# Threshold search for top-k attention: the last counting round shared by three engines, with a new instruction timetable

## What is computed

```python
top_k = max(1, int(s * 0.2))                      # s = 512, so 102
threshold = lax.top_k(scores, top_k)[0][..., -1:]
emphasis = jnp.where(scores >= threshold, 1.24, 1.0)
scores = scores * emphasis
```

## Time and profile before

| | |
|---|---|
| median of three runs | 2922.21 us |
| the profiled execution | 2924.21 us |
| its span | 2923.0 us |
| granted TensorE clock, mean | 0.874 of full speed |
| busy: PE, DVE, ACT, POOL | 75%, 80%, 50%, 41% |

### The profile page before, as it was taken

The page is one execution under the profiler, slowest core; times in us unless marked ns, Lnnn a source line. Parts: engine busy times, 40 slices in busy tenths (PEclk is TensorE's granted clock), DMA queues, the critical chain, the costliest instruction groups (busy, mean ns, idle before and its releaser), DMA issues.

```text
span 2923.0 us, 33653 instructions
## 1 busy us (share of the span) xinstructions
PE 2182.0 (75%) x8767; PEld 1101.9 (38%) x8767; DVE 2338.2 (80%) x6145; ACT 1463.2 (50%) x3124; POOL 1189.6 (41%) x1118
## 2 busy tenths in 40 slices
PE   4169776978778876888679876888769887778645
PEld 2016222553234522554235522454235532355214
DVE  5884898979898798978998798978989788953472
ACT  2406723766166733767056742757146751644323
POOL 2020253615454253725445152724445163724461
PEclk8589798999989998989989999989989898789757
DMA  4001112242043312233033321333133321313223
GB/s 107 0 15 36 29 37 85 80 107 75 27 122 71 104 50 72 91 96 93 27 107 75 105 60 54 109 78 103 31 97 83 101 63 39 113 38 111 83 75 95
DMA packets 137459, 215.11 MB, mean 74 GB/s; under 512 B 17872, under 2 KB 57440, under 8 KB 134112
## 3 DMA queue, kind: packets, MB, share of 16 engines
q1 hardware_dynamic: 133088, 203.88, 24.2%
q0 software_dynamic: 4096, 8.40, 0.9%
HBM read 190.06 MB, written 22.15 MB: 73 GB/s over the span
## 4 chain that ended last, share of the span: by engine, by line
DVE 35%; issue 19%; PE 19%; POOL 10%; ACT 9%; DVEq 4%; DMA 3%; SPq 1%; POOLq 0%; ACTq 0%
DVE wmask L804 10%; DVE best L946 6%; DVEq L948 4%; POOL gat L1649 4%; PE ps_att L1064 3%; ACT wmask L786 2%; POOL slots L1765 2%; PE ps_rest L1353 2%; PE ps_rest L1439 2%; PE ps_att L1075 2%; PE ps_rest L1792 1%; DVE pick L953 1%; POOL rest_c L1662 1%; POOL rest_c L1649 1%; DVE hg L1621 1%
## 5 line engine op out<-in xcount | busy, mean ns | idle before, releaser
L1413 POOL TENSOR_TENSOR gat<-sil,cbs 128x512 f32<-128x512 f32 x256 | 324.4, 1271 | 137.0 <-ACT sil L1378 74.2
L1378 ACT ACTIVATE sil<-ps_rest,w_b1T 128x512 f32<-128x512 f32 x256 | 175.3, 685 | 383.3 <-PE ps_rest L1353 369.9
L804 DVE TENSOR_SCALAR_CACHE_REDUCE wmask<-z,tc 128x512 bf16<-128x512 f16 x512 | 345.8, 742 | 18.3 <-ACT z L771 15.6
L980 POOL TENSOR_SCALAR wmask<-wmask 128x512 bf16<-128x512 bf16 x256 | 158.2, 618 | 412.4 <-DVE wmask L937 409.2
L1064 PE MATMUL ps_att<-z,Vp 128*32 128x128 f32 x2048 | 277.3, 280 | 13.1 <-DVE z L1136 13.1
L1353 PE MATMUL ps_rest<-rest_hT,WF 128*128 128x512 f32 x512 | 281.5, 636 | 0.0
L1343 PE MATMUL ps_rest<-gat,WP 128*128 128x512 f32 x512 | 269.3, 608 | 15.6 <-POOL gat L1413 15.4
L737 PE MATMUL ps_att<-qk 128*128 128x512 bf16 x512 | 227.8, 465 | 45.7 <-DMA qk<-bounce 27.1
L1064 PEld LDWEIGHTS ps_att<-z,Vp 128*32 128x32 f32 x2048 | 206.4, 111 | 124.5 <-issue 115.1
L1592 ACT ACTIVATE ps_rest<-cols,Aneg 128x512 f32<-128x512 f32 x256 | 173.3, 681 | 100.6 <-DVE hg L1621 91.2
L1075 PE MATMUL ps_att<-ident,z 128*128 128x128 f32 x1024 | 172.4, 293 | 63.6 <-ACT z L1093 40.1
(11 more groups left out here) (348 smaller groups left out, 4810.8 us busy)
## 6 DMA issues: line engine op xcount, KB each, us to landing
cbs<-spreads SPq DMA_DIRECT2D x128, 256.0 KB, 3.6
ccs<-spreads SPq DMA_DIRECT2D x128, 256.0 KB, 3.3
WF<-in_w SPq DMA_DIRECT2D x64, 256.0 KB, 2.7
WP<-in_w SPq DMA_DIRECT2D x64, 256.0 KB, 2.7
WF<-in_wfc SPq DMA_DIRECT2D x64, 256.0 KB, 2.7
WG<-in_wgate SPq DMA_DIRECT2D x64, 256.0 KB, 3.0
WP<-in_wproj SPq DMA_DIRECT2D x64, 256.0 KB, 3.1
qk<-bounce SPq DMA_DIRECT2D x32, 384.0 KB, 4.9
```

Source lines behind the costliest of these rows:

```text
L804: od.up(dve.tensor_scalar(wmask[:, i, :], z_at[i], tc[:, 0, i:i + 1], None, ALU.is_ge, ALU.add, accum_out=tc[:, 1, i:i + 1]))
L1413: weighed0.up(pool.tensor_tensor(gat[m % 2], sil[m % 2], cbs[e % 2][:], ALU.mult))
```

## The change

The last round is divided. VectorE compares and counts 20 tiles as before. GpSimd compares the other 12 (a new `pool_search`, at the end of each sample's part of the thread `pool_attention`) and writes the masks; ScalarE copies each of these masks onto itself with an accumulator output, which is its count. VectorE waits for all of ScalarE's results before it goes on. Rounds 0 to 2 stay as they are.

```diff
+SUMS = 12
-    aim, signed, counted = sig("aim", ROUNDS), sig("signed", sum(SIGNS)), sig("counted")
+    aim, signed, counted = sig("aim", ROUNDS), sig("signed", sum(SIGNS) + SUMS), sig("counted")
+    cut = sig("cut", SUMS)
...
+        for n in range(SUMS):
+            i = TILES - 1 - n
+            yield cut.at(b, n)
+            act.wait_ge(*cut.at(b, n))
+            signed.up(act.activation(wmask[:, i, :], wmask[:, i, :], ACT.Copy, accum_out=tc[:, 1, i:i + 1]))
+            yield 0.71
+
+    def pool_search(b):
+        yield aim.at(b, ROUNDS - 1)
+        pool.wait_ge(*aim.at(b, ROUNDS - 1))
+        for n in range(SUMS):
+            i = TILES - 1 - n
+            cut.up(pool.tensor_scalar(wmask[:, i, :], z_at[i], tc[:, 0, i:i + 1], None, ALU.is_ge))
+            yield 0.64
...
-            for i in range(TILES - SIGNS[k]):
+            for i in range(TILES - (SUMS if last else SIGNS[k])):
...
+            if last:
+                yield signed.all(b)
+                dve.wait_ge(*signed.all(b))
...
     def pool_attention():
         for b in every:
             yield from pool_prepare(b)
+            yield from pool_search(b)
```

The timetable is replaced as a whole, which can change the order of the instructions on every engine, though not what they are. `PERIOD` goes from 363.6 to 40.7 and `NEAR` from 0.135 to 0.172. The lines that matter most to the prediction, before and after:

```diff
-    "dve_rest": (110.8225, (2583.4, 3814.2, 3934.2)),
-    "pool_rest": (118.1500, (0.0, 1840.0, 357.8)),
-    "dve_attention": (104.6500, (5209.4, 3457.4, 3015.7)),
-    "pool_attention": (6.4600, (3316.0, 4230.4, 5170.6)),
...
+    "dve_rest": (104.6825, (5793.6, 8400.7, 6656.1)),
+    "pool_rest": (115.1100, (2051.6, 5258.8, 3995.7)),
+    "dve_attention": (93.0000, (10167.2, 8025.0, 7319.5)),
+    "pool_attention": (14.1400, (8487.7, 7453.4, 6623.6)),
```

More of the change, by code:

```diff
@@ new lines @@
+    "pe_rest": (155.6425, (4596.4, 4802.4, 4034.2)),
+    "act_rest": (81.6600, (7617.3, 5518.9, 6001.2)),
+    "dve_rest": (104.6825, (5793.6, 8400.7, 6656.1)),
+    "pool_rest": (115.1100, (2051.6, 5258.8, 3995.7)),
+    "sp_rest": (15.3000, (7423.3, 5306.0, 7908.4)),
+    "pe_mixtures": (10.3100, (5546.6, 7622.8, 7118.4)),
+    "act_mixtures": (2.7000, (9136.9, 5294.8, 7742.1)),
+    "dve_mixtures": (17.1800, (6046.7, 6325.1, 9511.1)),
+    "pool_mixtures": (3.1800, (9995.0, 13213.7, 14220.9)),
@@ new lines @@
+    "dve_finishes": (4.9600, (7588.8, 6320.2, 8481.6)),
+    "pool_finishes": (9.0400, (6613.1, 8359.1, 7703.0)),
+    "sp_finishes": (0.9000, (7836.7, 11917.1, 10957.7)),
+    "pe_choices": (42.2400, (3797.6, 2639.0, 4244.2)),
+    "act_choices": (2.5600, (10612.7, 11031.3, 6352.1)),
+    "dve_choices": (58.8100, (7707.6, 8274.7, 6414.2)),
+    "pool_choices": (20.4800, (10415.5, 10174.4, 11936.1)),
+    "pe_attention": (57.4700, (9896.4, 6022.6, 7715.0)),
+    "act_attention": (85.3400, (7827.1, 7989.3, 12072.6)),
@@ new lines @@
+    "dve_attention": (93.0000, (10167.2, 8025.0, 7319.5)),
+    "pool_attention": (14.1400, (8487.7, 7453.4, 6623.6)),
+    "sp_attention": (10.3500, (10326.0, 7186.8, 7219.5)),
+    "pe_prepares": (9.0800, (8305.0, 8950.2, 7552.3)),
+    "act_prepares": (2.9000, (4280.4, 6339.6, 0.0)),
+    "dve_prepares": (15.2500, (12159.1, 14307.4, 12682.8)),
+    "pe_refills": (12.8000, (9550.7, 8366.8, 10637.5)),
+    "act_refills": (19.2000, (3434.4, 6968.1, 4956.0)),
+    "sp_rows": (0.3937, (10974.6, 7967.1, 8988.0)),
@@ L80 @@
+    "sp_ups": (10.6875, (9315.3, 11200.4, 11649.4)),
+    "sp_downs": (7.0875, (8593.7, 8027.5, 6194.4)),
 }
@@ L487, in dve_norm @@
             od.up(dve.bn_stats(w.stats[:, j, :], src[:, j, :]))
-            yield 0.26
+            yield 0.22
         od.settle()
@@ L491, in dve_norm @@
             od.up(dve.bn_aggr(w.mv[:, j, :], w.stats[:, j, :]))
-            yield 0.13
+            yield 0.1
         od.settle()
@@ L500, in dve_norm @@
                                           ALU.subtract, ALU.mult))
-            yield 0.36
+            yield 0.3
     def pool_norm(w, b, k):
@@ L832, in dve_search @@
             od.up(dve.copy_predicated(hi_tc[:], under2, tc[:]))
-            yield 0.25
+            yield 0.14
             if k < 1:
@@ L987, in dve_guess @@
         aim.up(dve.memset(tc[:, 0, :], GUESS))
-        yield 0.3
+        yield 0.13
     def pe_rescale(b):
@@ L2139, in weave @@
             fresh.clear()
-    NEAR = 0.135
+    NEAR = 0.172
     sp_setup(); pool_setup(); act_setup(); pe_setup(); dve_setup()
```

67 lines of the change are left out of this document (21 added, 46 removed).

## The result

The changed kernel takes **2959.98 us** (median of four runs, 2958.95 to 2961.81) where the kernel before takes 2921.34 on the same chip: the ratio is 1.0127, with an interval of 1.0112 to 1.0142. It is 1.3% **slower**. The prediction, 2883 with a range of 2838 to 2925, was wrong in sign. The profiled execution is 2959.18, of which 2957.9 is the span (2923.0 before).

What follows compares the result with a forecast made beforehand. VectorE was taken as near full in the steady part, its eight last counting rounds all on the path. Gains of 24 (seven rounds), 8 (sample 0) and 7 us (clock) sum to 39: 2922.2 to 2883 us, range 2838 to 2925.

Steps and rivals of the forecast that it cites:

- Part 1: VectorE, last round: twelve counts of 0.67 us leave, 8.0 us a sample, leaving it 13.4 us.
- Part 2: GpSimd, last round: twelve compares at 0.70 us among six multiplications make 18.0 us; 24 us saved in seven samples.
- The bound above: GpSimd: a compare was taken to cost at most a multiplication of two tensors, 1271 ns.
- Six multiplications: GpSimd queue, last round: six expert multiplications of 1.35 us stand among the twelve compares, 8.1 us.
- the experts lose nothing: Experts beside the last round: six multiplications in 18.0 us where they had eight in 21.4 with a stop behind.
- Part 3: ScalarE, last round: sums of twelve masks, 8.4 us beside GpSimd; only the last, 0.9 us, on the path.
- Part 4: TensorE before the sum of `bad`: stop shrinks from 9 to about 2 us, clock stays up, 7 us together.
- Part 5: New timetable: changes no instruction's length; order alone bounded at 22 us either way, taken as 0.
- The compare is dear: Rival, GpSimd last round: compare at 1.35 us in the queue, round 25.8 us, total 2949; chance 0.10.
- VectorE ends the round: Rival, last round: at most two multiplications among the compares, 71 us gained, total 2851; chance 0.30.
- the third rival: GpSimd ends the last round with nine multiplications, 22.1 us; total 2919, no measurable change; chance 0.18.

Runs made afterwards that it cites:

- the probe: The kernel before with 12 groups of eight GpSimd instructions appended at its end, where nothing else runs, to read their lengths: 3065.89 us, a single run.
- the run with the cheap instruction: The changed kernel with GpSimd's twelve compares replaced by multiply-adds with two constants, last-round window test opened, so no sample is repaired: 2871.72 us (0.9842).
- the old timetable: The kernel before with the last round divided as in the change, its order kept and only the threads' total costs adjusted: 2955.68 us (1.0119).
- signs on twelve tiles: ScalarE counts twelve last-round tiles by Sign, GpSimd turns signs into masks; against the kernel before: 2913.26 us under its timetable, 2868.50 under the changed kernel's.
- the kernels with signs: ScalarE Sign counts, GpSimd mask conversions, timetable of the kernel before; twelve, fourteen and six tiles: 2913.26, 2909.64 and 2923.17 us.
- work it was not fitted to: The changed kernel's timetable with the last round left whole on VectorE, 3234.58 us, and with four tiles for GpSimd instead of twelve, 3310.01 us.

## Why the prediction was wrong, step by step

**Part 1, twelve counts leave VectorE: right.** The round of VectorE ends after 13.4 us (1397.12 to 1410.53), as forecast.

**Part 2, the price of the compare: this step failed.** The prediction put it as "I take L980, which has the compare's shape and its one tensor input", 0.62 us and 0.70 in the queue. It measured 1.55 and 1.54. The bound above, the multiplication of two tensors at 1.27, was broken too: it took for granted that a second input can only add to the price, and the probe shows one-input forms at 1.49 to 1.92. L980 has the shape but not the form; it multiplies and adds with two constants, and it is the exception. The prediction had put the point from which a dear compare decides at 0.98 in the queue; 1.54 lies far beyond it.

The rest of part 2 held. Six multiplications were forecast among the compares and seven came, in the change and in the run with the cheap instruction. The weave's length works out by the same sum with the right price: 12 x 1.54 + 7 x 1.25 + 0.8 for the last sum is 28.0, and the trace has 1397.10 to 1425.07, 28.0. One small term was wrong in it: instructions back to back in this queue start 0.59 apart when one lasts 0.61 (1.18 for the two at 1680.23) and 1.25 apart when one lasts 1.26, so there is no 0.08 for each on top. With the cheap instruction the round is 16.8 for the 18.0 forecast, and the whole kernel 2872 for 2883. So the mechanism of the forecast was right and one price in it was wrong; that price had twelve places in each of eight rounds. That the experts lose nothing by the division held in the change as well (their end comes 62.1 us after `bad` for 62.9), but not under the old timetable, as the table shows.

**Part 3, ScalarE's sums: right.** 0.629 and 0.186 us, 0.82 together where 0.9 was taken.

**Part 4, the shorter stop of TensorE: right in the stop, not in its fruit.** The stop before the sum of `bad` is 1.77 us for 8.98, near the 2 forecast. But the pair of up matmuls behind it still takes 2.08. The timeline of TensorE, and the windows before and behind that point:

```profile
1418.44 1.13 PE L1362 MATMUL ps_rest<-gat,WP 128*128 128x512 f32 x2 [2.33 <-POOL gat L1432]
1419.40 1.02 PE L1372 MATMUL ps_rest<-rest_hT,WF 128*128 128x512 f32 x2
1422.74 1.13 PE L1362 MATMUL ps_rest<-gat,WP 128*128 128x512 f32 x2 [2.32 <-POOL gat L1432]
1425.63 0.27 PE L881 MATMUL ps_att<-g_bad,ones_col 128*1 128x32 f32 x2 [1.77 <-DVE g_bad L846]
1425.83 2.08 PE L1372 MATMUL ps_rest<-rest_hT,WF 128*128 128x512 f32 x2
```

```profile
1421.00:1425.50 4.50, 1.13 (x2) 0.30 (x2) 0.39 (x3) 2.54 (x6) 4.46 (x4) 0.92 0.00 0
1425.50:1430.00 4.50, 3.79 (x8) 1.32 (x10) 3.01 (x15) 0.74 (x2) 1.26 (x1) 0.50 0.00 0
```

The dear compares starve TensorE all through the round: it stands 2.3 us before each of the last two pairs of down matmuls and is busy for 1.13 of the 4.50 us before the sum, and then the clock is at 0.50. The prediction looked at one stop where the row before it mattered as well. With the cheap instruction the stops are 0.18 and 0.82 us, the same pair takes 1.12, and the window has 1.00 on both sides:

```profile
1695.38 1.13 PE L1362 MATMUL ps_rest<-gat,WP 128*128 128x512 f32 x2 [0.18 <-POOL gat L1432]
1697.32 0.22 PE L881 MATMUL ps_att<-g_bad,ones_col 128*1 128x32 f32 x2 [0.82 <-DVE g_bad L846]
1697.47 1.12 PE L1372 MATMUL ps_rest<-rest_hT,WF 128*128 128x512 f32 x2
```

```profile
1692.80:1697.30 4.50, 3.53 (x8) 1.05 (x6) 1.37 (x7) 3.46 (x9) 4.34 (x6) 1.00 0.25 80
1697.30:1701.80 4.50, 2.97 (x12) 1.34 (x13) 3.02 (x15) 0.69 (x1) 1.26 (x1) 1.00 0.01 2
```

So this term too hung on the price of part 2.

**Part 5, the timetable at nothing: near for this change, and its bound wrong.** With the division it makes no difference that can be told (2955.68 under the old one, 2959.98 under the new, and the intervals of the two ratios overlap). But 22 us is not what order alone can do. With signs on twelve tiles the same replacement gains 45 us (2913.26 to 2868.50), and with the last round left whole on VectorE it costs 314. The bound was taken from the finish as it stands in the trace before, eight instructions of 5.36 us together; in the kernels with signs one of them took up to 14.45 us. So "it changes no instruction's length" failed too: about 20 of the 45 us are the two rounds in which a finish held VectorE under the old order. The timetable has no worth of its own; it has one for each kernel.

**The rivals.** "The compare is dear" had the place and the way right and the price still too low, 1.35 in the queue for 1.54, so it gave 2949 for 2960; it had 0.10. Its own round, 25.8 us, had the six multiplications of the forecast. The reason for so small a chance was L980, an instruction alike in shape. The Trainium skill had spoken for it (GPSIMD Engine Reference, "Performance pitfalls for Q7 kernels"), with the slower loop of a comparison. It pointed the right way, but this case doesn't bear out its reason: in the probe a multiplication by a constant takes the same 1.487 us as a comparison's 1.486. "VectorE ends the round" needed at most two multiplications, and seven came; the third rival had nine at the price of L980. The range left the dear compare out, and so left out the result.

## What to carry to other kernels

Price a moved instruction by a row with the same operation and the same kinds of operands, not by one with the same shape; where the trace has none, a group of eight at the end of the kernel gives the price in one run, and until then the bound above is no bound. If an engine is dear for an operation, look which half of the work it is cheap for: here ScalarE's Sign gives the count, and GpSimd's multiply-add the mask. A timetable fitted to one set of steps is part of that kernel: judge a division of work under a fitted plan, and when a shorter round gives nothing, look at what runs beside the choice and now ends after it, and at single instructions far longer than their median: a queue that is filled without a gap on one engine can hold a step of another.

## What the runs showed that was not expected

- On GpSimd, with nothing beside it, one instruction on 128x512 elements in 16 bits takes 613 ns as a multiplication and an addition with two constants, 1487 ns as the multiplication alone, and 1917 ns as a multiplication and a maximum. More work in one instruction can be the faster form. The one-input compare at 1.55 us costs more than the product of two float32 tensors at 1.27.
- A step of the finish on VectorE, 0.35 us in the median, took 14.3 us while GpSimd's instructions followed each other without a gap. Such a run costs nothing as long as no finish falls into it: in the changed kernel GpSimd's queue is unbroken for 27 us in seven of the rounds, and the longest finish there took 1.37.
- TensorE's clock did not fall at the same point behind two stops of like length. In the change it is at 0.50 when the pair behind a stop of 1.77 us starts, with two stops of 2.3 before that one. In the kernel with signs on twelve tiles under the new timetable the stop is 2.15, the pairs shown before it follow each other without one, and the pair behind it takes 1.12 at full clock. The clock falls there too, but 2.6 us after the restart, as the two windows show, and its 6.8 us at 0.50 lie in the choice.

```profile
1684.30 1.13 PE L1378 MATMUL ps_rest<-gat,WP 128*128 128x512 f32 x2
1685.26 1.02 PE L1388 MATMUL ps_rest<-rest_hT,WF 128*128 128x512 f32 x2
1688.44 0.22 PE L893 MATMUL ps_att<-g_bad,ones_col 128*1 128x32 f32 x2 [2.15 <-DVE g_bad L851]
1688.59 1.12 PE L1378 MATMUL ps_rest<-gat,WP 128*128 128x512 f32 x2
```

```profile
1688.40:1691.20 2.80, 1.27 (x4) 0.38 (x4) 2.57 (x8) 0.00 (x0) 2.63 (x4) 1.00 0.00 0
1691.20:1698.00 6.80, 5.75 (x10) 2.08 (x10) 4.68 (x16) 0.69 (x1) 2.12 (x3) 0.50 0.00 1
```

- The changed timetable on work it was not fitted to costs 11% and 13% against the kernel before (3234.58 and 3310.01), though it removes and adds no instruction.
